# Adjacency rows loaded on ScalarE's DMA queue, each behind the row sum that frees its buffer

## The reference

```python
# layer 1: graph convolution, two products with the same normalised matrix
A = adj + I
d = rsqrt(A.sum(axis=1))            # row sums
An = d[:, None] * A * d[None, :]
x = layernorm(x + An @ (relu(An @ (x @ W1) + b1) @ W2) + b2)
# layer 2: two attention heads, masked with adj > 0 or the diagonal
h = norm(x) @ ff0[i].T
e = where(mask, leaky_relu(s_src[:, None] + s_dst[None, :]), -9e15)
att = norm(softmax(e, axis=1) @ h + norm_input)
out = layernorm(x + sum_i elu(att @ ff1[i].T) / 2)
```

## Time and profile before

| | |
|---|---|
| median of 3 runs | 1058.78 us (1058.07 to 1059.05) |
| the profiled execution | 1058.95 us, of which the span is 1057.2 us |
| TensorE matmuls busy | 988.1 us, 93% |
| VectorE busy | 698.4 us, 66% |
| ScalarE busy | 495.6 us, 47% |
| mean granted TensorE clock | 0.975 |
| bytes moved | 226 MB, mean 214 GB/s |

### The profile page before, as it was taken

How to read it: one execution, slowest core, us unless ns; L and a number is a source line. 1 busy time by engine, 2 the same in 40 slices (tenths; PEclk the granted TensorE clock), 3 DMA queues, 4 the chain that set the end, 5 groups by cost and what they waited for, 6 DMA issues and landing times. The chain is left out here.

```text
span 1057.2 us, 9226 instructions
## 1 busy us (share of the span) xinstructions
PE 988.1 (93%) x2592; PEld 477.7 (45%) x2592; DVE 698.4 (66%) x1249; ACT 495.6 (47%) x709; POOL 114.5 (11%) x146
## 2 busy tenths in 40 slices
PE   5788999999999999999869999999999999999992
PEld 4333444444644444444655444444544444454541
DVE  0567766654355433444828767788779999888977
ACT  3433332211200000001257765879668698878773
POOL 0011111111040000000710000101010101001012
PEclk8999999999999999999869999999999999999997
DMA  9999999999386999996023132222222232222211
GB/s 350 428 426 426 427 428 424 425 423 381 133 307 249 380 375 377 381 381 249 1 61 100 60 100 67 68 95 70 89 70 81 89 100 90 100 70 91 90 50 40
DMA packets 62219, 226.03 MB, mean 214 GB/s; under 512 B 4513, under 2 KB 44129, under 8 KB 52065
## 3 DMA queue, kind: packets, MB, share of 16 engines
q1 hardware_dynamic: 57056, 208.56, 51.4%
q10 hardware_dynamic: 5120, 17.01, 4.0%
HBM read 205.59 MB, written 19.96 MB: 213 GB/s over the span
## 5 line engine op out<-in xcount | busy, mean ns | idle before, releaser
L1200 PE MATMUL ps<-colbuf,stat 128*128 128x512 f32 x992 | 439.0, 598 | 27.3 <-DVE diag L760 26.8
L1200 PE MATMUL ps<-T,Yw 128*128 128x512 f32 x1024 | 446.8, 595 | 11.1 <-DVE T L918 11.1
L918 DVE SCALAR_TENSOR_TENSOR T<-T,mring 128x2048 f32<-128x2048 f32 x128 | 292.8, 2289 | 70.4 <-ACT T L577 69.9
L577 ACT ACTIVATE T<-Rrow,small,ratio 128x1024 f32<-128x1024 f32 x256 | 301.2, 1230 | 67.7 <-PE ps L1200 67.5
L1200 PEld LDWEIGHTS ps<-T,Yw 128*128 128x128 f32 x1024 | 194.7, 191 | 249.1 <-issue 229.6
L1200 PEld LDWEIGHTS ps<-colbuf,stat 128*128 128x128 f32 x992 | 186.4, 191 | 249.9 <-issue 219.3
L497 ACT ACTIVATE W<-W 128x4096 f32<-128x4096 f32 (+30 forms) x32 | 66.1, 2067 | 147.1 <-DMA W<-in_adj 147.1
L516 ACT ACTIVATE stat<-xw_g 128x128 f32 (+1 forms) x32 | 9.9, 310 | 197.8 <-PE ps L1200 155.9
L799 DVE TENSOR_SCALAR mtile<-colbuf 128x4096 uint8<-128x4096 f32 x30 | 69.7, 2322 | 10.4 <-DMA mask<-mtile 8.3
L795 DVE TENSOR_TENSOR colbuf<-colbuf,ident 128x128 f32 (+1 forms) x26 | 7.6, 292 | 91.8 <-DMA colbuf<-in_adjT 91.8
L720 DVE TENSOR_TENSOR W<-W,colbuf 128x3712 f32<-128x3712 f32 (+28 forms) x29 | 62.3, 2148 | 0.1
(11 more groups left out here) (161 smaller groups left out, 590.3 us busy)
## 6 DMA issues: line engine op xcount, KB each, us to landing
colbuf<-in_adjT SPq DMA_DIRECT2D x58, 2048.0 KB, 12.9
mring<-mask SPq DMA_DIRECT2D x128, 256.0 KB, 2.6
mask<-mtile ACTq DMA_DIRECT2D x32, 512.0 KB, 10.0
Rrow<-s_src SPq DMA_DIRECT2D x9, 512.0 KB, 4.3
W<-in_adj SPq DMA_DIRECT2D x2, 2048.0 KB, 14.9
W<-in_adjT SPq DMA_DIRECT2D x2, 2048.0 KB, 13.3
out<-final SPq DMA_DIRECT2D x5, 512.0 KB, 4.1
W<-in_xT SPq DMA_DIRECT2D x8, 256.0 KB, 6.8
```

The costliest lines, as they stand in the source:

```text
L577: last = act.activation(T[:, c % TS, j, :], Rrow[:, g % 2, :], ACT.Relu, scale=ratio[:, c * JB + j:c * JB + j + 1], bias=small[:, 8:9])
L918: v.scalar_tensor_tensor(out=tile, in0=tile, scalar=1.0, in1=mring[:, c % TS, :, :].rearrange("p b n -> p (b n)"), op0=ALU.add, op1=ALU.mu ...
L1200: return pe.matmul(*args, skip_group_check=True, **kw)
```

## The change

Row load b leaves the loop of SyncE. Row loads 0 and 1 are issued by ScalarE right behind its three small loads at the start, row load b + 2 right behind row sum b, before ScalarE's wait for `deg_ready`. The wait in front of a row load is the same count as before. SyncE's loop holds only the tile loads (and `weights`); a tile load no longer stands behind a wait for a row sum.

```diff
--- before.py
+++ after.py
@@ -313,9 +313,7 @@
             for k in range(NG):
                 sp.dma_start(xT0[:, cols(k, GW)], t["xT"][:, cols(k, GW)]).then_inc(x_loaded[k], 16)
             for b in range(B):
-                u, lo = b % RING, ROW_FROM[b] * P
-                sp.wait_ge(rowsum_done, b + 1)
-                sp.dma_start(rowbuf[:, u % 2, lo:], adj_rows[b, :, lo:]).then_inc(row_loaded[u % 2], 16)
+                u = b % RING
                 sp.wait_ge(pe_block, b + 1)
                 if b >= RING:
                     sp.wait_ge(colacc_done, b - RING + 1)
@@ -483,6 +481,14 @@
             act.dma_start(w1[:, :], t["W1"]).then_inc(first_loaded, 16)
             for dst, src in BIASES:
                 act.dma_start(dst, src).then_inc(biases_loaded, 16)
+
+            def load_row(b):
+                lo = ROW_FROM[b] * P
+                act.wait_ge(rowsum_done, b + 1)
+                act.dma_start(rowbuf[:, b % 2, lo:], adj_rows[b, :, lo:]).then_inc(row_loaded[b % 2], 16)
+
+            for b in range(2):
+                load_row(b)
             act.wait_ge(zeros_ready, 3)
             act.activation(small[:, 10:11], small[:, 9:10], ACT.Sqrt)
             for s in range(SN):
@@ -495,6 +501,8 @@
                 act.wait_ge(row_loaded[b % 2], 16 * (b // 2 + 1))
                 row = rowbuf[:, b % 2, ROW_FROM[b] * P:]
                 act.activation(row, row, ACT.Copy, accum_out=rowpart[:, b % 2:b % 2 + 1]).then_inc(rowsum_done, 1)
+                if b + 2 < B:
+                    load_row(b + 2)
                 act.wait_ge(deg_ready, b + 1)
                 act.activation(small[:, 3:4], small[:, 1:2], ACT.Sqrt).then_inc(root_ready, 1)
```

## The result

| | median of the runs | profiled execution |
|---|---|---|
| before | 1058.78 us (1057.34 to 1059.10, 5 runs) | span 1057.2 |
| after | 1064.85 us (1063.39 to 1066.38, 5 runs) | span 1063.0 |

The ratio is 1.0057 with a 95% interval of 1.0045 to 1.0070: 6.1 us slower. The prediction was 1059.6 with 1062.6 as its upper end, so it was wrong in the time and in the cause.

What follows compares the result with a forecast made beforehand. Full DMA engines bound stage 1, TensorE's last wait there deciding. Issue cost 0, late tiles +1.4, start -0.6 gave +0.8 on 1058.95, 1059.75; the median lies 0.17 lower, so 1059.6 us, 8-in-10 range 1056.8 to 1062.6.

Steps and rivals of the forecast that it cites:

- What bounds, and the due times: TensorE's last stage 1 wait decides; at 7.09 us a block, blocks 17 and 18 are due at 172.10 and 179.19.
- Issues on ScalarE at no cost: Row issues on ScalarE, 0.33 us each, hide in its 0.49 us idle before the square root: 0 us.
- Packets in turn: Two queues sharing the DMA engines get packets one for one, whatever their size, so row b + 1 and tile b finish together.
- The start: First row loads share engines with x: row sum 0 at 23.9, row sum 2 at 39.4, 2.1 us late; time term -0.6.
- The weights give 3.8 us back: Weights opposite row 5, packet for packet: rows gain 1.64 MB, 3.8 us, so row 6 comes before its old time.
- The middle, "late tiles +1.4": Tiles landing with row b + 1 make blocks 17 and 18 start 1.4 and 1.3 us past due; likeliest case, 0.48.
- The signs: Expected VectorE tile waits in blocks 14 to 18; wrong if row sums between 80 and 170 us moved over 3 us.
- Rows overtake tiles: Rival: engines share by bytes, rows run one or two ahead and delay block 17's tile; 1061.9 or 1064.2 us; chance 0.19.
- Faster: Rival: a fuller start gives up to 4 of 5 us, rows and tiles both early; -2.6, 1056.2 us; chance 0.15.
- Nothing changes: Rival: tiles in the middle keep their 0.7 lead or a stall falls elsewhere, terms cancel; 1058.8 us; chance 0.18.

Runs made afterwards that it cites:

- e2: Changed kernel, but row loads 0 and 1 stay on SyncE's queue, only later row loads on ScalarE's; 1061.41 us, ratio 1.0032.
- e1: Changed kernel, but SyncE again waits for row sum b - 2 before it issues tile load b; 1064.02 us, ratio 1.0049.
- e4: Changed kernel, but the 452 KB of weights follow tile 20 instead of tile 4; 1064.20 us, ratio 1.0056.
- e9: Changed kernel, but the weights are two loads of 226 KB, behind tiles 4 and 5; 1062.83 us, ratio 1.0048.
- e5: Changed kernel, but row loads 0 and 1 stay on SyncE and the weights follow tile 20 instead of tile 4; 1059.84 us, ratio 1.0015.
- e11: Changed kernel, but row loads 0 and 1 stay on SyncE and the weights follow tile 29; 1058.97 us, ratio 1.0006.
- e3: Kernel before, but row loads 0 and 1 are issued on ScalarE's queue behind its three small loads; 1061.04 us, ratio 1.0028.
- e12: Changed kernel, but ScalarE waits for the last piece of x before it issues row loads 0 and 1; 1064.79 us, ratio 1.0052.
- e8: Kernel before, but the two bias loads follow ScalarE's first copies and TensorE waits for them just ahead of block 0; 1058.01 us, ratio 0.9996.
- e10: Kernel before, but with weights behind tile 20 and the two bias loads behind ScalarE's first copies; 1056.96 us, ratio 0.9990.
- e7: Kernel before, but the weights follow tile 20 instead of tile 4; 1057.26 us, ratio 0.9989.

## Why the prediction was wrong, step by step

*What bounds, and the due times: right in the main.* The blocks from 20 on ran at 7.09 us, and the 5.9 us at block 30 went through to the span. But the run of waits ends at block 14 already, in both kernels (149.41 before, 155.42 after); behind it TensorE waits only 0.47 us before (block 18) and 0.18 us after (block 19).

*Issues on ScalarE at no cost: right*, 0.49 us of idle time before the square root as before.

*Packets in turn: right between equal packets*, 238 against 237, and right beside x (154 against 152 between 10 and 16 us). It failed beside the weights, see below.

*The start: this step failed, in two of its terms.* "Row sum 2 can start at 39.4": it started at 44.54. Row sum 0 came at 25.88 and not at 23.9 (2.0 us; by its own terms, 21 + 2.6, the prediction's figure should have been 23.6). I took over from the kernel before that SyncE's queue has moved 607 packets by 8 us. Here it was fewer (0 to 8 us, after), as row packets moved beside x from 6 us on:

```profile
q1 hardware_dynamic: 441, 0.82, 40.5%
```

And row load 2 took 14.9 us from issue to sum, not 11.8: I took the two ends of a small load into idle engines, 2.0 us. But at 33.0, 3.4 us after the issue, it had not moved a packet. What the tiles already had in the engines went first: that this is the reason is inferred. In e2 the same load, issued at 20.77 beside tiles, had moved none by 24.2, also 3.4 us; in e1, where the engines were running dry, it was issued at 31.36 and moved by 33.1, 1.7 us. So 2.25 tiles went ahead where I had 1.7.

*The weights give 3.8 us back: mis-sized, and its rule failed there.* From row 3 to row 5 it was 2.4 us (7.4 to 5.0). The working is also off by its own rule: 1.64 MB is the difference between a tile and the weights opposite a row. The kernel that has a tile there is e4, and its lateness fell by 1.8 us over the same rows, so by this pair the relief is 0.6 us and not 3.8. (Against the old order, which carries the weights too, the rule would give a whole tile, 4.9 us.) What I took for granted is that the row queue moves a packet for each one of the weights. While most of the weights moved, 58 to 62 us after, it did not:

```profile
q1 hardware_dynamic: 147, 1.02, 60.7%
q10 hardware_dynamic: 63, 0.69, 40.7%
```

147 packets went against 63. Why the row queue took fewer turns there no run shows. That such a load still brings the rows something, e9 and the pair e2 and e5 show (from row 4 to row 6 the rows of e2 gained 2.7 us, those of e5 1.1, so 1.6 by this pair).

The three differences are 2.0 + 3.1 + 1.4 = 6.5 us; that is nearly the gap between row sum 6 at -1.7 as I had it and +5.0 as it came, 6.7, as it must be when the terms are read one after the other.

*The middle, "late tiles +1.4": the wrong side.* I held that the delay of the start is gone by row 6 and that only landings of tiles decide. I also held that row b + 1 lands with tile b. What came was row b with tile b: the lead of one tile, 2.1 MB, counted above at row sum 17, is 4.9 of the 6.0 us there. A lead of the tiles is no reserve that rows can draw on. With turns by packet it stays, so the late side was the rows. This phase, in whole transfers, is what the kernel lacks a rule for: in the loop of before each row load stood ahead of its tile. e2 shows the opposite phase, rows early and `diag` 3.8 us late for tiles, e5 and e11 the phase between. The state that the prediction describes came about, nearly, in e5: `diag` of block 17 is 1.1 us late for tiles, and the time is 1059.84 us.

*The signs.* Row sums between 80 and 170 us came 5 to 6 us late, more than the 3 us at which the prediction calls itself wrong, and VectorE did not wait for tiles in blocks 14 to 18. ScalarE's wait for row loads did get shorter (87.0 against 96.3 us).

*The rivals.* "Rows overtake tiles" had the right sign and nearly the right time (1061.9 to 1064.2), and the wrong actor: the tiles overtook the rows. "Faster" assumed that the row loads make the start fuller; 181 GB/s against 190. "Nothing changes" fell with the 6.1 us. e1, e3 and e12 show that neither the gate nor x is the whole of it: whoever waits for row sum 0 leaves either idle engines (2.2 to 2.5 us) or a lead of the other queue.

What stays open: how the 3.4 us of entry split, why the row queue took 63 packets against 147 beside the weights, and where the steps of up to 1 us come from.

## What to carry to other kernels

Where the DMA engines are full, one queue is also an order: it says which of two streams lands first. Putting the streams on two queues gives that up; they then take turns by packet, and here a lead that one got while the other's queue was empty stayed for more than 130 us, so find out who is ahead at the first point where both have work. Work out what the consumer needs first, row or tile, before taking a wait out from between them, and on one queue move small loads out of a stretch that is short of bytes; on two queues they also shift the lead (e4, e9).

## What the runs showed of the hardware

A row load issued on an empty queue, while the engines were busy with 16 KB packets of another queue, had moved nothing 3.4 us after its issue (after and e2); with the engines running dry it took 1.7 us (e1). Two queues with 16 KB packets moved 238 against 237 of them, and 16 KB beside 2 KB packets 154 against 152; beside the 3.6 KB packets of the weights it was 63 against 147, so one packet for one does not hold for every pair. Without the two small loads that spread one line over 128 partitions, the first 9 us moved 236 GB/s (e8) and 249 (e10) instead of 190 (before) and 187 (e7).
